# Routing and expert phases of a two-layer transformer: down projection behind the next chunk's first slice, and an expert's short tile in column groups

## The reference

```python
def _L0_ffn_ref(hidden_states, gate_weight, Wg, Wu, Wd, Ws_g, Ws_u, Ws_d):   # E = 16
    x = hidden_states.reshape(n, d)                       # n = 8240, d = 192
    scores = jax.nn.sigmoid(x @ gate_weight.T)
    capacity = math.ceil(n / E * TOP_K)                   # 1030
    topk_score, topk_ids = jax.lax.top_k(scores.T, capacity)
    xg = x[topk_ids]
    gate = jax.nn.silu(jnp.einsum('ecd,efd->ecf', xg, Wg))   # f = 768
    up = jnp.einsum('ecd,efd->ecf', xg, Wu)
    out = jnp.einsum('ecf,edf->ecd', gate * up, Wd)
    out = out * topk_score[..., None]
    y = jnp.zeros((n, d), x.dtype).at[topk_ids.reshape(-1)].add(out.reshape(-1, d))
    shared = jax.nn.silu(hidden_states @ Ws_g.T) * (hidden_states @ Ws_u.T) @ Ws_d.T   # f = 384
    return y.reshape(b, l, d) + shared
```

## Time and profile before

| | |
|---|---|
| median of 3 runs | 4267.86 us (4261.8 to 4270.67) |
| the profiled execution, its own time | 4265.64 us |
| its span | 4263.8 us |
| mean granted TensorE clock | 0.949 of full speed |
| PE busy | 3833.5 us, 90% |
| PEld busy | 2300.0 us, 54% |
| DVE busy | 2471.8 us, 58% |
| ACT busy | 1472.8 us, 35% |
| POOL busy | 1316.0 us, 31% |
| bit loop | 469.1 to 609.0 us of the span |
| list loop | 630.8 to 787.3 us |
| experts, from the first slice on | 812.5 to 1695.8 us |

### The profile page before, as it was taken

The page is one execution under the profiler, slowest core; times in us unless marked ns, Lnnn a source line. Parts: engine busy times, 40 slices in busy tenths (PEclk is TensorE's granted clock), DMA queues, the critical chain, the costliest instruction groups (busy, mean ns, idle before and its releaser), DMA issues. The chain is left out here.

```text
span 4263.8 us, 74517 instructions
## 1 busy us (share of the span) xinstructions
PE 3833.5 (90%) x23747; PEld 2300.0 (54%) x23747; DVE 2471.8 (58%) x4668; ACT 1472.8 (35%) x2946; POOL 1316.0 (31%) x1533
## 2 busy tenths in 40 slices
PE   8899878799999999675999999999997879799998
PEld 8788545466666666343233333333333556577776
DVE  1567568522222222687887787777784557644443
ACT  0122124211111111243577777777775111111111
POOL 0212013244444443466000000001000221177776
PEclk9999999899999999776799999999999989999999
DMA  6222111333333321246433233333324632277775
GB/s 229 63 59 62 42 39 44 101 65 64 64 64 64 62 62 20 75 148 161 61 47 47 47 47 47 47 53 49 53 36 112 162 100 44 74 171 172 173 172 120
DMA packets 336727, 354.00 MB, mean 83 GB/s; under 512 B 53036, under 2 KB 298084, under 8 KB 335024
## 3 DMA queue, kind: packets, MB, share of 16 engines
q1 hardware_dynamic: 251999, 268.42, 25.9%
q0 software_dynamic: 62272, 62.25, 9.5%
q10 hardware_dynamic: 22288, 20.93, 1.6%
HBM read 241.18 MB, written 110.47 MB: 82 GB/s over the span
## 5 line engine op out<-in xcount | busy, mean ns | idle before, releaser
L2221 DVE TENSOR_REDUCE at_mx<-psum 128x1 f32<-128x998 f32 (+1 forms) x768 | 885.1, 1190 | 231.8 <-PE psum L2034 228.7
L2176 ACT ACTIVATE at_p<-psum 128x512 f32<-128x512 f32 (+3 forms) x1536 | 851.9, 588 | 301.3 <-PE psum L2108 271.5
L2108 PE MATMUL psum<-at_q,at_k 99*128 99x512 bf16 (+3 forms) x1536 | 521.5, 382 | 20.4 <-issue 15.3
L2034 PE MATMUL psum<-at_k,at_q 96*128 96x512 bf16 (+3 forms) x1536 | 475.6, 392 | 51.9 <-DVE at_mxl L2228 19.8
L2094 PE MATMUL psum<-at_p,at_v 128*32 128x486 f32 (+3 forms) x3072 | 407.1, 602 | 0.3 <-ACT at_o L2166 0.3
L1259 ACT ACTIVATE ex_silu<-psum 128x384 f32<-128x384 f32 (+1 forms) x288 | 131.8, 458 | 767.1 <-PE psum L1203 573.1
L1291 DVE TENSOR_TENSOR ex_hT<-ex_silu,psum 128x384 f32<-128x384 f32 (+1 forms) x288 | 147.6, 513 | 419.2 <-ACT ex_silu L1259 229.2
L2108 PEld LDWEIGHTS psum<-at_q,at_k 99*128 99x128 bf16 (+1 forms) x1536 | 155.5, 102 | 425.7 <-ACT at_p L2176 269.1
L1807 POOL DMA_DIRECT2D recips<-at_shares x24 | 12.8, 535 | 1036.7 <-DVE at_mx L2221 772.0
L1225 PE MATMUL psum<-ex_wd,ex_hT 128*128 128x192 f32 (+1 forms) x1728 | 291.5, 327 | 0.0
L1225 PEld LDWEIGHTS psum<-ex_wd,ex_hT 128*128 128x128 f32 (+1 forms) x1728 | 264.1, 179 | 15.9 <-issue 3.6
(11 more groups left out here) (403 smaller groups left out, 6984.9 us busy)
## 6 DMA issues: line engine op xcount, KB each, us to landing
mx_wd<-in_e_dT SPq DMA_DIRECT2D x72, 288.0 KB
qk_parts<-hd_parts SPq DMA_DIRECT2D x32, 579.4 KB
at_k<-qk_parts SPq DMA_DIRECT2D x144, 128.8 KB, 4.8
at_q<-qk_parts SPq DMA_DIRECT2D x144, 124.8 KB, 4.6
tok_p<-in_x SPq DMA_DIRECT2D x12, 1176.0 KB, 14.6
mx_wg<-in_e_gT SPq DMA_DIRECT2D x72, 192.0 KB
mx_wu<-in_e_uT SPq DMA_DIRECT2D x72, 192.0 KB
v_rows<-hd_v_out SPq DMA_DIRECT2D x8, 1536.0 KB
```

Of the source, the lines that this page charges most:

```text
L2034: mm = pe.matmul(psum[0:ctx_rows[t], 3 + 2 * ((PRO + n) % 2) + k, 0:w], Q[v][0:R6, j * 1024 + 128 * t:j * 1024 + 128 * t + ctx_rows[t]], K ...
L2108: pe.matmul(psum[0:n, i % RING, 0:w], K[u][:, j, 128 * t:128 * t + n], Q[u][:, j * 1024 + at:j * 1024 + at + w], start=True, stop=True).th ...
L2176: act.activation(P[0:n, c % 2, j, 0:w], psum[0:n, i % RING, 0:w], ACT.Exp).then_inc(exp_ready, 1)
L2221: dve.tensor_reduce(mx[0:ctx_rows[t], j * CT + t:j * CT + t + 1], pair(n)[0:ctx_rows[t], 0:CTX], AX_X, ALU.max).then_inc(s_free, 1)
```

## The change

In the route phase the down projection of a chunk moves behind the first slice of the next chunk, in both loops, so that the pairs of banks now go by (half + f) % 2 and both loops are unrolled by two. `xr` gets two halves and is filled one chunk earlier. In the bit loop a slice comes ahead of the first count sum (f = 1), another (f = 2) ahead of the second, and the next chunk's f = 0 ahead of the down projection; VectorE makes the row sums of the chunk before behind the first try, and the third product comes ahead of the third try. In the list loop product 0 comes ahead of the hit, product 1 behind it, product 2 behind the first quarter, and ScalarE's SiLU calls follow that order; GpSimd's score stores are spread over the `pair_up` calls. In the expert phase the six matmuls of the short tile write to four column groups (PSUM lanes 0, 32, 64, 96), two groups with two matmuls each; VectorE copies the four shares out, adds them and scales them, behind the second product of the next expert.

```diff
-        xr = sb("sh_xr", [128, W4])
+        xr = sb("sh_xr", [128, 2, W4])
...
-            def pair_up(j):
-                pool.wait_ge(u_full, j * FC)
+            def pair_up(j, half):
+                if not isinstance(j, int) or j > 1:
+                    pool.wait_ge(u_full, j * FC - FC)
...
+                if c + LOOPS + 2 < 2 * LOOPS:
+                    pair_up(c + LOOPS + 2, c % 2)
...
-                pe.wait_ge(hT_ready, j * FC + max(f - 1, 0))
-                gate, lift = psum[:, 2 * (f % 2), 0:W4], psum[:, 2 * (f % 2) + 1, 0:W4]
+                if not isinstance(j, int) or j * FC + f > 1:
+                    pe.wait_ge(hT_ready, j * FC + (f - 1))
+                pair = (half + f) % 2
+                gate, lift = psum[:, 2 * pair, 0:W4], psum[:, 2 * pair + 1, 0:W4]
...
-                shared_up(pe, j, (0,))
+                shared_up(pe, j, half, (1,))
                 total(0)
-                shared_up(pe, j, (1,))
+                shared_up(pe, j, half, (2,))
                 total(1)
-                shared_up(pe, j, (2,))
+                if following:
+                    shared_up(pe, j + 1, 1 - half, (0,))
                 shared_down(pe, j, (0,))
                 total(2)
                 shared_down(pe, j, (1,))
...
+            def chunk(c, half, following=True):
+                j = c + LOOPS + 1
+                shared_up(pe, j, 1 - half, (1, 2))
+                list_rows(c, half)
+                if following:
+                    shared_up(pe, j + 1, half, (0,))
+                shared_down(pe, j)
...
                 act.activation(hot_hi[:, half, :, HB2:2 * HB2], hit[:], ACT.Copy, scale=row[:, 0:1])
-                shared_silu(act, c + LOOPS, (1,))
+                shared_silu(act, c + LOOPS, half, (2,))
...
                 try_bit(0)
-                shared_mult(dve, j, (0,))
+                if not first:
+                    shared_rows(dve, j - 1)
+                shared_mult(dve, j, half, (0,))
                 keep_bit(0)
                 try_bit(1)
-                shared_mult(dve, j, (1,))
+                shared_mult(dve, j, half, (1,))
                 keep_bit(1)
+                shared_mult(dve, j, half, (2,))
                 try_bit(2)
-                shared_mult(dve, j, (2,))
                 keep_bit(2)
-                shared_rows(dve, j)
...
+                shared_mult(dve, c + LOOPS, half, (0,))
                 if not first:
                     dve.wait_ge(hot_used, c - 1)
...
+                shared_mult(dve, c + LOOPS, half, (1,))
+                for k in range(4):
+                    low = dve.tensor_tensor(hot_lo[:, half, k * 32:(k + 1) * 32, :],
...
+                    if k == 0:
+                        shared_mult(dve, c + LOOPS, half, (2,))
+                low.then_inc(lo_ready, 1)
                 shared_rows(dve, c + LOOPS)
...
+        shares = sb("ex_shares", [SHORT, GROUPS, D])
+        short = sb("ex_short", [SHORT, D])
...
-                    for t, n in tiles:
+                    if p == NP - 1:
+                        for f in range(FC):
+                            g = f % GROUPS
+                            mm = pe.matmul(psum[32 * g:32 * g + SHORT, 4 + p % 2, 0:D],
+                                           hT[:, f, 128 * LAST:128 * LAST + SHORT], wd[:, half, f, :],
+                                           start=(f < GROUPS), stop=(f + GROUPS >= FC), skip_group_check=True)
+                    for t, n in tiles if p < NP - 1 else ():
...
+            def short_rows(e, half):
+                for g in range(GROUPS):
+                    last = dve.tensor_copy(shares[:, g, :], psum[32 * g:32 * g + SHORT, 4 + (NP - 1) % 2, 0:D])
+                last.then_inc(shares_ready, 1)
+                dve.wait_ge(shares_ready, e + 1)
+                dve.tensor_reduce(short[:], shares[:].rearrange("n g d -> n d g"), AX_X, ALU.add).then_inc(short_ready, 1)
+                dve.wait_ge(short_ready, e + 1)
+                dve.tensor_scalar(ys[0:SHORT, half, LAST, :], short[:], score[0:SHORT, half, LAST:LAST + 1], None, ALU.mult) \
+                    .then_inc(ys_ready, 1)
...
+                        if j == 1 and (not isinstance(n_used, int) or n_used):
+                            short_rows(e - 1, 1 - half)
...
+            dve.wait_ge(used[1], E0 // 2)
+            short_rows(E0 - 1, 1)
```

More of the change, by code:

```diff
@@ L723, in _, with shared_up @@
                         .then_inc(scores_out, 16)
-            with pool.Fori(LOOPS + 1, 2 * LOOPS) as j:
-                pair_up(j)
+                if c + LOOPS + 2 < 2 * LOOPS:
+                    pair_up(c + LOOPS + 2, c % 2)
             pool.wait_ge(scores_out, 32 * NC)
-        def shared_up(pe, j, slices=range(FC)):
+        def shared_up(pe, j, half, slices):
             toks = x_flat[:, 0, bass.ds(j * W4, W4)]
@@ L743, in remainder @@
                 def remainder(first):
-                    g = pe.matmul(gate, wr[0:64, cols], xr[0:64], start=first, stop=not first)
-                    u = pe.matmul(lift, wr[64:128, cols], xr[64:128], start=first, stop=not first)
+                    g = pe.matmul(gate, wr[0:64, cols], xr[0:64, half], start=first, stop=not first)
+                    u = pe.matmul(lift, wr[64:128, cols], xr[64:128, half], start=first, stop=not first)
                     return g, u
@@ L782, in _, with bits @@
             pe.wait_ge(score_ready, 3)
-            with pe.Fori(0, LOOPS) as j:
+            shared_up(pe, 0, 0, (0,))
+            def bits(j, half, following=True):
                 def total(s):
@@ L796, in _ @@
                 shared_down(pe, j, (1,))
+            with pe.Fori(0, LOOPS // 2 - 1) as i:
+                for half in range(2):
+                    bits(i * 2 + half, half)
+            bits(LOOPS - 2, 0)
+            bits(LOOPS - 1, 1, False)
             def sums(n, weights, rhs, bank):
@@ L857, in _ @@
                 act.activation(score[:, s * W4:s * W4 + n], psum[:, s, 0:n], ACT.Sigmoid).then_inc(score_ready, 1)
-            with act.Fori(0, LOOPS) as j:
-                shared_silu(act, j)
+            with act.Fori(0, LOOPS // 2) as i:
+                for half in range(2):
+                    shared_silu(act, i * 2 + half, half, range(FC))
             for n, dst in enumerate((hiT, loT, scT)):
@@ L875, in high_digits, with chunk, shared_mult @@
                 last.then_inc(hot_ready, 1)
-            with act.Fori(0, NC // 2) as i:
-                for half in range(2):
-                    c = i * 2 + half
-                    shared_silu(act, c + LOOPS, (0,))
-                    high_digits(c, half)
-                    shared_silu(act, c + LOOPS, (2,))
-        def shared_mult(dve, j, slices=range(FC)):
+            def chunk(c, half, following=True):
+                shared_silu(act, c + LOOPS, half, (1,))
+                high_digits(c, half)
+                if following:
+                    shared_silu(act, c + (LOOPS + 1), 1 - half, (0,))
+            shared_silu(act, LOOPS, 0, (0,))
+            with act.Fori(0, NC // 2 - 1) as i:
+                for half in range(2):
+                    chunk(i * 2 + half, half)
+            chunk(NC - 2, 0)
+            chunk(NC - 1, 1, False)
+        def shared_mult(dve, j, half, slices):
             dve.wait_ge(d_full, j * 2)
@@ L921, in _, with bits @@
             dve.wait_ge(score_ready, 3)
-            with dve.Fori(0, LOOPS) as j:
+            def bits(j, half, first=False):
                 def try_bit(s):
@@ L1062, in phase_experts @@
     NP = len(PAIRS)
+    LAST, SHORT = ES[-1]
+    GROUPS = 4
+    assert LAST == 2 * (NP - 1) and SHORT <= 32 and FC > GROUPS
     with ExitStack() as ctx:
@@ L1287, in hidden @@
                         dve.wait_ge(u_full, e * UP + (j + 1))
-                        if j == 0:
+                        if j == 0 and (not isinstance(n_used, int) or n_used):
                             dve.wait_ge(used[1 - half], n_used)
```

83 lines of the change are left out of this document (41 added, 42 removed).

## The result

The changed kernel takes **4233.02 us** (median of 4 runs, 4228.4 to 4237.59), the kernel before 4268.32 us (4 runs): ratio 0.9917, interval 0.9902 to 0.9931. Forecast were 4214 us and 4206 to 4228. The direction is right, the time lies above the range. The profiled execution took 4228.7 us, span 4226.9; before they were 4265.64 and 4263.8. So of the 19 us above the forecast the profile holds 15.1 (4228.7 against 4213.6), and the rest is how far the median lies above the profiled execution, 4.3 us here where 0.4 was added.

A forecast was written before the change was run, and what follows sets the result against it. TensorE bounds the experts; in the bit and list loops the order of work leaves waits. Savings of 19.0 + 13.5 + 19.5 = 52.0 us from the profiled 4265.64 give 4213.6, said as 4214; range 4206 to 4228.

The forecast's parts named there:

- part 3: Experts: short tile's six matmuls become four waves in column groups, 1.30 us less in each of 15 experts, 19.5 us.
- Cover enough, by 0.1 us: cost nothing: Experts, VectorE: copies, reduction and scaling take 2.7 us; the third product ends at 932.7, before TensorE's fifth slice at 932.89.
- my bound of 6: Experts: most the added VectorE sums would cost, 0.4 x 15 us, if each of six operations is 0.08 slower.
- rival (a): Experts: VectorE's sums take 4.1 us instead of 2.7 and take back the groups' gain; 4233, half-way 4223; chance 0.14.
- The attention row: Profile row pricing the experts' column groups: 8 records in two waves of four groups, 0.84 us, 0.42 a wave.
- rival (c): Experts: column groups overlap less, a quarter more per wave, saving 17 us, time 4216; chance 0.05.
- rival (d): Experts: TensorE granted a lower clock for part of each expert; at 0.92 they cost 75 us more, 4289; chance 0.03.
- Part 1: Bit loop: both TensorE waits go, pass 13.91 to 11.9 us, saving 19.0; next late would be product 2, 0.1 in hand.
- the bound of 17.9: Bit loop: lower bound of the saving, in us, if product 2 is 0.1 late each time.
- Part 2: List loop: VectorE is the bound and its 1.39 us wait on the second down half goes; 13.5 us, bounds 10 and 15.
- Rival (b): Route loops give half: VectorE's or ScalarE's order brings waits of 0.8 us a pass, twenty passes; 4230; chance 0.08.
- Rival (e): Whole change: counts bound the bit loop, groups serialise, only part 2 or less is left; within 0.2%, 4262; chance 0.02.

The follow-up runs named there:

- Experiment 4: Changed kernel with the four shares laid so that the numbers to be added lie side by side; 4224.97 us, ratio 0.9905.
- experiment 2: Changed kernel with three column groups (shares) instead of four; 4220.44 us, ratio 0.9886.
- short first: Changed kernel with three shares and the 6-row tile gathered first of the nine instead of last; 4205.88 us, ratio 0.9862.
- experiment 9: Changed kernel run once more, unaltered, on another occasion; 4225.66 us, ratio to before 0.9902.
- (18): Changed kernel, four shares, with the short tile's scatter sent behind the next expert's gathers, so these run in their old place; 4268.72 us, ratio 0.9985.

## Why the prediction was wrong

**The step that failed** is in part 3: "Cover enough, by 0.1 us: cost nothing". The term was the reduction. I took its price per element from a row whose elements lie side by side (753 ns for 576) and wrote 950 for 768; the reduction of the change reads its four shares at a step of 192 elements and takes 1470. Experiment 4 shows the same 768 at 941 when they lie side by side, experiment 2 the wait gone with three shares. The wait is 54.21 - 53.71 = 0.50 us per expert, 7.5 us in all: above my bound of 6 and below the 9.8 of rival (a)'s half-way case. The six operations take 3.3 us, half-way between my 2.7 and rival (a)'s 4.1. Its 4233 for the whole time is met by chance, since its sums were to take back all 19.5. I had given it 0.14, and had written that there was no row of such a reduction. A term with 0.1 us in hand, a price from an unlike row and a factor of fifteen needed its bound in the range. The range that I gave for the forecast, 4207 to 4220, left even the bound of 6 out: its upper end is 4265.64 less 17.9 + 10 + 17 alone. Its lower end was misadded too, since 20 + 15 + 19.5 + 2 gives 4209.

**Part 3, the groups.** Right: 1.30 us less per expert forecast; the short tile itself takes 2.04 - 0.75 = 1.29 us less, and without the wait 55.00 - 53.71 = 1.29. The attention row was the right one to price a wave by, and rival (c) is out. The first expert did not give its share: 0.06 us instead of 1.30, as TensorE's clock rose 2.5 us later in it than before. That is rival (d) in small, in a place that no part of the sum looked at.

**The late signals** were no term. In the trace of before they were there to read, a SiLU 1.7 us behind its gate in each expert and 0.33 us between 55.33 and 55.00; I had seen the period and not asked what ended it. Expert 14 shows that its delay of 1.1 us cost nothing: 55.00 is also 53.71 + 1.29. Here the late signals cost the changed kernel 14 x (54.61 - 54.21) = 5.6 us and before 14 x 0.30 = 4.2: 1.4 us of the gap. So 19.5 forecast - 7.5 (wait) - 1.4 (late signals) - 1.2 (first expert) leaves 9.4; 9.2 was measured to the next phase's start.

**Part 1**, 16.9 for 19.0: a pass of 12.14, not 11.9. The slices between other tiles take 2.45 and 2.47 instead of 2.37, the sums with the second half 0.1 more, and the middle sum the 0.28 of its late product, less what the other sums were shorter (0.14 for 0.25). That term was named with "about 0.1 us in hand"; the bound of 17.9 was still too high. **Part 2**, 12.8 for 13.5: right, with the bound that was named. Rival (b) would have cost 16 us; 2.8 were lost.

**The rest**: the unchanged phases gave 1.6 and took 3.4 us. The seven later phases took 2555.6, 2559.1 and 2559.5 us in the three profiles of before and 2559.0, 2551.2, 2548.2 and 2547.4 in the four of the changed kernel. So executions of one kernel differ there by up to 12 us, and a single profile's total is no better than that. The changed kernel's mean is 6.6 us lower; whether the change has a part in that is not shown. Rival (e) is out, and (d) as it was priced, with a clock of 1.00 over fourteen experts.

On the occasion without late signals the changed kernel took 4215.66 us, near the forecast, but for other reasons: the experts' 54.21 still hold the wait, and the unchanged phases were 7 us shorter.

**What beats both kernels:** three shares. Beside the changed kernel on one occasion it took 4218.86 against 4225.66 us (their intervals to before overlap), and its experts are shorter by 0.5 us or more, with late signals and without. The gathers back in their old place add nothing without late signals, and with four shares they lost 23 us against the changed kernel on the same occasion (4268.72 against 4245.32) when these were strong. The 4205.88 of "short first" had no late signals and no changed kernel beside it, and its experts take the 53.71 of its two neighbours, so it is not shown to be better.

## What to carry to other kernels

Price an added operation by a row with the same access pattern, not only the same kind and size; where cover ends within a tenth of a microsecond and a loop multiplies it, treat the cover as absent. Choose the number of column groups that divides the matmuls: beyond that a group adds only sums. And before an odd wait is explained by an edit, run the unaltered kernel again beside it: three edits seemed to cure what stayed away from an unedited kernel too.

## What the runs showed of the hardware

- **Step and price on VectorE.** Six lanes, float32: reduction of 768 elements side by side 941 ns, at a step of 192 over four shares 1470, 576 over three shares at the same step 802. A copy of 192 elements out of PSUM takes 349 ns, written at a step of four 493. The Trainium skill (SBUF — State Buffer, Door 1: The DMA port swizzle) says that SBUF has lines of 16 bytes, that an access to a new line costs, and gives four float32 as how far one can step for free. That a far step costs agrees with 1470 against 941; a step of exactly four was not free for the copies, 493 against 349.
- **Late signals.** On some occasions a SiLU starts up to 3.8 us after its gate matmuls have ended (0.04 us otherwise), one to three times per expert, and on others never, for all kernels of an occasion alike: 13 profiles have them, 7 don't. They move with GpSimd's nine gathers: the latest is at the seventh or eighth slice where these end 16.1 or 16.7 us into the expert, at the tenth where they end at 21.6 to 22.7, at the twelfth where they end at 25.5. VectorE's product is 0.3 to 1.7 us late as well in some experts. They cost 0.3 to 4.0 us per expert. In runs without a profile only the strongest show beyond the spread: the medians of before are 4265 and 4266 us on the occasions without them, 4267 to 4268 on three with them and 4279 to 4282 on the last. Code loading is not the cause: between 900 and 1600 us, where most of them fall, the queues for instructions moved three packets in the changed kernel (the view of transfers):

```profile
q8 instruction: 2, 0.03, 0.0%
q14 instruction: 1, 0.01, 0.0%
```

In the profiles without late signals, all but one, the view of transfers also gives the weights' landing times, and in none with them; whether that has the same cause I can't say. What the late signals are, and why on one occasion the kernel with its gathers in their old place lost 3.95 us per expert and before 0.62, stays open; the runs show only that the place, the kernel and the occasion all enter.
- **The clock behind an idle stretch.** In the 25 us ahead of the first expert TensorE is busy 5.7 us, and the first slice runs at a granted clock of 0.50. In the profile after the change the clock rose 5.4 us later, in that of experiment 9, the same kernel, 2.7 us later; the first expert took 56.34 and 55.02 us. In (18) it fell inside ten experts, behind waits such as the 2.80 us of expert 3, and cost 1.3 us in each.
